# Issuing the dense products with the known block between the small scaling products, in the Schur and assembling stages

## The reference, cut to what matters

```python
def step(S, qkv):
    Qc, Kc, Vc = qkv
    G = Kc.T @ Kc + RIDGE_EPS * I
    W = jnp.linalg.solve(G, Kc.T @ Vc)
    U = U0
    for _ in range(POWER_K):
        U, _ = jnp.linalg.qr(W @ U)
    Wr = U @ (U.T @ W)
    S_new = DECAY_ALPHA * S + Wr
    out = SCALE * (Qc @ S_new)
    return (S_new, out)
```

## Time and profile before

| | before |
|---|---|
| device time, median of 3 runs | 1335.05 us (1333.93 to 1336.13) |
| device time of the profiled execution | 1337.31 us |
| its span in the trace | 1335.5 us |
| mean granted TensorE clock over the span | 0.866 of full |
| PE busy, share of the span | 74% |
| DVE busy | 84% |
| ACT busy | 50% |

### The profile page before, as it was taken

How to read it: one execution, slowest core, us unless ns; L and a number is a source line. 1 busy time by engine, 2 the same in 40 slices (tenths; PEclk the granted TensorE clock), 3 DMA queues, 4 the chain that set the end, 5 groups by cost and what they waited for, 6 DMA issues and landing times.

```text
span 1335.5 us, 41205 instructions
## 1 busy us (share of the span) xinstructions
PE 989.9 (74%) x17632; PEld 762.0 (57%) x17632; DVE 1118.0 (84%) x3452; ACT 661.8 (50%) x1392; POOL 174.6 (13%) x118
## 2 busy tenths in 40 slices
PE   1693017596687899897899897782499838998597
PEld 0463016555576667776767777672477625765254
DVE  6875996699999599999599999689889699764996
ACT  3683017555344567645467645352246515655254
POOL 2420123201011001011001111001200020001000
PEclk9897558798688899899799899796699958999799
DMA  4321003300000001110002110013112100111001
GB/s 149 104 99 38 0 0 129 127 25 17 3 4 3 3 18 33 35 51 3 4 10 73 34 36 3 4 31 129 33 36 71 51 30 18 48 48 32 8 17 32
DMA packets 42693, 53.04 MB, mean 40 GB/s; under 512 B 2992, under 2 KB 25600, under 8 KB 42512
## 3 DMA queue, kind: packets, MB, share of 16 engines
q1 hardware_dynamic: 42512, 50.42, 11.4%
HBM read 32.53 MB, written 17.87 MB: 38 GB/s over the span
## 4 chain that ended last, share of the span: by engine, by line
PE 54%; DVE 31%; ACT 9%; issue 4%; POOL 1%; DMA 0%; DVEq 0%; ACTq 0%; POOLq 0%
PE a_bank L547 7%; PE a_bank L618 6%; PE a_bank L707 5%; DVE a_outer L1564 4%; DVE a_total L1570 4%; DVE a_outer L1568 4%; DVE a_blocks L1573 4%; PE a_bank L713 3%; PE a_bank L697 3%; PE a_bank L561 3%; PE a_bank L832 3%; PE a_bank L817 3%; PE a_bank L799 3%; PE a_bank L643 2%; PE a_bank L769 2%
## 5 line engine op out<-in xcount | busy, mean ns | idle before, releaser
L987 ACT ACTIVATE a_work<-a_bank 128x512 f32<-128x512 f32 (+1 forms) x193 | 109.3, 606 | 180.9 <-PE a_bank L675 138.5
L1487 POOL TENSOR_TENSOR a_root<-a_recip,a_half 128x32 f32<-128x32 f32 (+2 forms) x24 | 89.8, 3742 | 592.7 <-DVEq L1559 575.2
L675 PE MATMUL a_bank<-a_ident,a_blocks 128*128 128x128 f32 x256 | 38.5, 318 | 134.6 <-DVE a_blocks L1584 134.6
L1564 DVE TENSOR_TENSOR a_outer<-a_blocks,a_weight 128x62 f32<-128x62 f32 (+15 forms) x248 | 129.6, 523 | 0.0
L1570 DVE TENSOR_REDUCE a_total<-a_outer 128x62 f32<-128x62 f32 (+30 forms) x248 | 127.2, 513 | 0.3
L987 ACT ACTIVATE a_solve<-a_bank 128x512 f32<-128x512 f32 (+2 forms) x184 | 88.0, 526 | 69.2 <-PE a_bank L713 52.9
L1568 DVE TENSOR_TENSOR a_outer<-a_blocks 128x60 f32<-128x60 f32 (+14 forms) x240 | 119.4, 497 | 0.0
L1573 DVE TENSOR_TENSOR a_blocks<-a_blocks,a_outer 128x60 f32<-128x60 f32 (+14 forms) x240 | 118.6, 494 | 0.0
L675 PEld LDWEIGHTS a_bank<-a_ident,a_blocks 128*128 128x128 f32 x256 | 37.1, 203 | 135.5 <-DVE a_blocks L1584 135.5
L618 PE MATMUL a_bank<-a_scaled,a_blocks 128*128 128x352 f32 x256 | 92.6, 505 | 13.1 <-ACT a_blocks L987 13.1
L987 ACT ACTIVATE a_scaled<-a_bank 128x512 f32<-128x512 f32 (+2 forms) x133 | 66.8, 528 | 57.9 <-PE a_bank L697 46.2
(11 more groups left out here) (198 smaller groups left out, 2232.0 us busy)
## 6 DMA issues: line engine op xcount, KB each, us to landing
a_pair<-in_L_attn_x SPq DMA_DIRECT2D x16, 256.0 KB, 3.0
s_base<-a_pair SPq DMA_DIRECT2D x16, 256.0 KB, 2.8
s_xnt<-a_xb SPq DMA_DIRECT2D x12, 256.0 KB, 2.0
s_c<-a_xc SPq DMA_DIRECT2D x12, 256.0 KB, 2.6
a_cg<-s_c SPq DMA_DIRECT2D x12, 256.0 KB, 2.8
a_cc<-s_c SPq DMA_DIRECT2D x12, 256.0 KB, 3.4
a_blocks<-s_base SPq DMA_DIRECT2D x12, 256.0 KB, 3.4
s_x<-a_xc SPq DMA_DIRECT2D x12, 256.0 KB, 2.0
```

The source lines that it names most:

```text
L987: nc.scalar.activation(out, view, ACT.Copy, scale=scale).then_inc(emptied, 1)
L1487: nc.gpsimd.tensor_tensor(root[:, :, a:b], recip[:, :, a:b], half[:, :, a:b], ALU.pow).then_inc(roots_ok, 1)
L1564: known = ch.inc(V.tensor_tensor(terms, m[:, :, i:HB, 0:i], bcast(weight[:, :, 0:i], 2, n_i), ALU.mult))
```

## The change

`scale_rows` and `squares` of the Tensor class become one generator, `solved`, that both stages use. For k = 0, 1, 2 the four dense products of part k (`known_into`) are no longer issued in one piece after the scaling of part k+1, but one at a time inside it: after its 16th, 32nd and 48th small product, and after its last. The dense products of the last part still come in one piece, since no scaling is left. Each dense product now takes its bank by itself, so it waits for that one bank instead of for four. The scaling of part k+1, the dense products and the squares of part k are now one step without a `yield` inside it (also on ACT, where one `yield` goes), so woven stages are cut in fewer, larger pieces. No product is added or removed.

```diff
@@ class Tensor
-            def scale_rows(self, k, stationary, moving):
...
-            def squares(self, k, half, mask, known):
-
-                four = self.u.fill(4, apart=True)
-                for c in range(4):
...
+            def solved(self, stationary, moving, half, mask, known):
...
+                def known_into(k, c):
+                    bank = self.u.fill(apart=True)
                     at = 32 * k + 8 * c
...
+                def scale(k, before):
+                    two, four = self.u.fill(2, apart=True), []
+                    for i in range(8):
+                        for c in range(4):
+                            for s in range(2):
+                                q = 32 * k + 8 * c + i
+                                last = nc.tensor.matmul(two[s][HB * c:HB * c + HB, i * DH:(i + 1) * DH], stationary(s, q), moving(s, q),
+                                                        start=True, stop=True)
+                        if before is not None and i % 2 == 1 and i < 7:
+                            four.append(known_into(before, i // 2))
+                    last.then_inc(filled, 2)
+                    if before is not None:
+                        four.append(known_into(before, 3))
+                    return four
+
+                mark = self.u.n + 2
+                scale(0, None)
+                yield
+                for k in range(parts):
+                    ready = mark
+                    if k + 1 < parts:
+                        mark = self.u.n + 2
+                        four = scale(k + 1, k)
+                    else:
+                        four = [known_into(k, c) for c in range(4)]
+                    self.u.need(ready, apart=True)
...
+                    last.then_inc(filled, 4)
+                    yield
                 return self.u.mark()
...
@@ class Scalar, solved
                 for k in range(NQ // 32):
                     if k + 1 < NQ // 32:
                         self.scale_rows(k + 1)
-                        yield
                     self.squares(k, dst, scale)
                     yield
```

More of the change, by code:

```diff
@@ L688, in lead_return @@
                 self.at["lead"] = self.u.mark()
-            def scale_rows(self, k, stationary, moving):
-                two = self.u.fill(2, apart=True)
-                for i in range(8):
-                    for c in range(4):
-                        for s in range(2):
-                            q = 32 * k + 8 * c + i
-                            last = nc.tensor.matmul(two[s][HB * c:HB * c + HB, i * DH:(i + 1) * DH], stationary(s, q), moving(s, q),
-                                                    start=True, stop=True)
-                last.then_inc(filled, 2)
-                return self.u.mark()
@@ L702, in squares @@
-            def squares(self, k, half, mask, known):
-                four = self.u.fill(4, apart=True)
-                for c in range(4):
+            def solved(self, stationary, moving, half, mask, known):
+                parts = NQ // 32
+                def known_into(k, c):
+                    bank = self.u.fill(apart=True)
                     at = 32 * k + 8 * c
-                    nc.tensor.matmul(four[c][:].rearrange("p (q z c) -> p q z c", z=2, c=HB)[:, :, half], mask[:], known[:, at:at + 8, :],
+                    nc.tensor.matmul(bank[:].rearrange("p (q z c) -> p q z c", z=2, c=HB)[:, :, half], mask[:], known[:, at:at + 8, :],
@@ L708, in squares @@
                                      start=True, stop=False, skip_group_check=True)
-                for i in range(8):
-                    for c in range(4):
-                        for s in range(2):
-                            both = scaled[HB * c:HB * c + HB, (2 * k + s) * 8 + i, :]
-                            last = nc.tensor.matmul(four[c][rows(s, None), i * DH:(i + 1) * DH], both, both, start=False, stop=True,
-                                                    skip_group_check=True)
@@ L715, in squares @@
-                last.then_inc(filled, 4)
+                    return bank
+                def scale(k, before):
[12 more added lines that the diff above has]
+                    return four
@@ new lines, in solved @@
+                mark = self.u.n + 2
[9 more added lines that the diff above has]
+                    self.u.need(ready, apart=True)
+                    for i in range(8):
+                        for c in range(4):
+                            for s in range(2):
+                                both = scaled[HB * c:HB * c + HB, (2 * k + s) * 8 + i, :]
+                                last = nc.tensor.matmul(four[c][rows(s, None), i * DH:(i + 1) * DH], both, both, start=False, stop=True,
+                                                        skip_group_check=True)
+                    last.then_inc(filled, 4)
+                    yield
@@ L745, in assemble @@
                 self.pe.sem_inc(schur_read, 1)
[L747 to L759 removed]
+                yield from self.solved(lambda s, q: work[rows(s, 1), q, :], lambda s, q: beside(kept[rows(s, 1), q, :], eyes[1][rows(s, 1)]),
+                                       0, minus[0], kept)
             def moments(self, src, mark):
```

25 lines of the change are left out of this document (2 added, 23 removed).

## The result

| | before | after |
|---|---|---|
| device time, median | 1335.59 us (1333.93 to 1339.07) | 1371.64 us (1364.94 to 1377.77) |
| device time of the profiled execution | 1337.31 us | 1374.81 us |
| mean granted clock over the span | 0.866 | 0.855 |

The ratio is 1.0265, with a 95% interval of 1.0208 to 1.0323: slower by 2.1 to 3.2%. The direction was forecast, the size was not: 1371.64 lies above the range of 1330 to 1366, and next to the time of the rival "Half clock holds", 1373.

A forecast was written before the change was run, and what follows sets the result against it. No engine bounds the whole; PE limits six stages, through code fetching (floor 7.2 us a part) and clock. 1337.31 + 0 + 14 (woven stages) = 1351.3, less 2.26 for the median: 1349 us, range 1330 to 1366.

The forecast's parts named there:

- Half clock holds: Rival: without long dense runs the clock stays down in straight and woven stages; +38 us, 1373 us; chance 0.13.
- the separate waits for each bank ... add no stop: At the dense products: the awaited banks were emptied by ACT during squares or first scaling products, so no cost.
- the sum of 14 us: Woven stages `assemble(1)` to `assemble(3)`: 3.15 + 2.2 + 0.8 - 1.5 = 4.65 us a stage, 14 us for three.
- the changes of shape: Entering, starting and leaving a dense run costs 0.35 us at full clock, 0.53 at half; three more a part.
- The wait for `xa`: Woven stages, first step c of `write`: a new wait of 2.2 us for ACT's copies.
- The 0.8 us: Woven stages, third step c of `write`: a new wait of 0.8 us behind ACT's copies of the second squares.
- The relief of 1.5 us: Woven stages: dense products ahead of the first stop and waits for ACT cover code fetching; -1.5 us a stage.
- I take the middle ... no change: Straight stages `schur(1)` to `schur(3)`: 30.6 us each, between full and half clock, beside 30.2 now.
- the bound of 4.5: Straight stages: upper end of the range, +4.5 us a stage. At half clock, last dense run and squares also 4.5.
- 9.4 was worked out: Straight stages: a part's work at half clock with the change takes 9.4 us, over the code floor of 7.2.
- `schur(0)` and `lead_return` took up what lay ahead of them: Gains or losses in `assemble(0)` and `schur(0)` go into PE's waits for DVE and count as nothing.
- The stops at the scaling line: Stops for "issue" should shrink in `assemble(1)` to `assemble(3)` and remain in the straight stages.

The follow-up runs named there:

- e11: Changed kernel with each part's four dense products in one run behind the scaling and one wait for all four banks; 12.4 us over the kernel before.
- e8: Changed kernel with dense products in one run and the `yield` back on both engines, so only the separate bank waits are left; 8.3 us over before.
- e12: Kernel before with three more copies of an already met wait, each with its semaphore increment, ahead of dense runs; 9.9 us over before.
- e1: Changed kernel with each part's four dense products in one run behind the scaling, separate bank waits and new `write` order kept; 20.0 us over before.
- e10: Changed kernel with `write` in one piece behind `assemble` in the last three assembling stages; 58.8 us over the kernel before.
- e9: Kernel before with `write` in one piece behind `assemble` in the last three assembling stages; 43.8 us over the kernel before.
- the halves: Two kernels, the change in the Schur stages alone and in the assembling stages alone; 12.2 and 18.9 us over the kernel before.
- e2: The change in the Schur stages alone, assembling stages as in the kernel before; 12.2 us over before.
- e4: Changed kernel with every dense product issued twice, the second overwriting the first; 44.5 us over the kernel before.
- e7: The change in the Schur stages alone, with the four dense products in one run after the scaling's 32nd small product; 8.9 us over before.

## Why the prediction was wrong, point by point

**What the loss is made of.** The order of `write` alone is 12.4 us (e11). The separate waits are 8.3 (e8) or 9.9 (e12) in kernels that spread nothing; the 7.6 between e1 and e11 agree, but the two intervals overlap. The spreading is 15.4 between the changed kernel and e1, 15.0 - 8 = 7 between e10 and e9, and some 10 from the halves (12.2 + 18.9 - 12.4 - 8.3). So 12 + 8 + 7 to 15 makes 27 to 35 of the 35.4. That the parts add up is assumed in this; the upper end comes out by itself, since 12.4 + 7.6 + 15.4 is the way from before over e11 and e1 to the changed kernel.

**A step that failed: "the separate waits for each bank ... add no stop".** I looked at whether the banks were free, and but for one wait of 1.3 us in `assemble(0)` they were. In kernels that spread nothing, the waits cost 8 to 10 us all the same. No rival had this.

**The woven stages: the sum of 14 us had no term for the clock.** It took the 0.92 of the earlier trace rows as given. The three stages lost 25.0 us by the profile. Of this the new waits for ACT are 6.7 us (2.11 + 1.24 + 1.24 at L897, 3 x 0.69 at L892; forecast 9.0), the changes of shape 27 x 0.22 = 5.9 at full clock (forecast 9.45), and the stops for "issue" gave back 9.8 - 6.6 = 3.2 (forecast 4.5). Each of these terms was forecast too high, and they leave some 16 us that the sum did not have. The clocks over the stages fell from 0.91, 0.88 and 0.92 to 0.80, 0.77 and 0.89; that this is where the 16 us went is shown in pieces for e11 only, in one stage.

**The order of `write`, priced without the clock.** The wait for `xa` was right: 2.2 us forecast for the first stage, 2.11 measured. In the trace after:

```profile
560.77 2.12 PE L732 MATMUL a_bank<-a_scaled 32*64 32x64 f32 x128
562.82 1.09 PE L883 MATMUL a_bank<-a_ident,a_xa 128*128 128x128 f32 x8
566.03 2.07 PE L897 MATMUL a_bank<-a_xa,a_xc 128*128 128x128 f32 x8 [2.11 <-ACT a_xa L983]
```

On ACT the copies that PE waited for:

```profile
562.93 2.06 ACT L983 ACTIVATE a_pair<-a_bank 128x512 f32<-128x512 f32 x4 [2.05 <-PE a_bank L732]
564.85 1.12 ACT L983 ACTIVATE a_xa<-a_bank 128x512 f32<-128x512 f32 x2
```

2.11 us at L897 in `assemble(1)` and 1.24 in the other two, and one more wait of 0.69 at L892. The 0.8 us that the prediction had for this one is 0.5 by its own rows (2.7 less two steps of about 1.1), and the copies of the squares, which were to hold it up, had ended before; PE waited for the copy of its own products, 0.60 us on ACT. What was missing is the clock: 4.15 us in e11's `assemble(1)`, in which PE fell to half clock once more behind the new wait. The relief of 1.5 us needs dense products ahead of the first stop, and e11 has none there (2.71 us). So its 12.4 us (7.7 to 17.1) stand against 3.0 a stage, 9.0 in all, which the interval includes.

**The straight stages: "I take the middle ... no change" failed.** They came out at +4.3 us each by the profile, beside the bound of 4.5; the two other profiles of the same Schur stages have +2.5 (e2) and +1.7 (e10), and the timed e2, with its waits, 12.2 in all. Where the mix of single dense and small products ran at half clock, its parts took 9.2 to 10.6 us (875.66 to 895.13 and 656.32 to 676.73 in the trace after), where 9.4 was worked out; what failed was the choice between the clocks. The bound itself was too low by its own rows: the last dense run and squares at half clock are 3.71 + 2.0 = 5.7 us, not 4.5. That the clock is a large part is shown by e4; e7 against e2 shows the clock, but no difference in time. How much spreading takes of the straight stages varies: 10.7 against e1, 6.0 between e10 and e9. In the changed kernel the last two straight stages have 2.4 and 1.2 us of stops for code left, where the kernel before had 4.2 and 5.0; my reading, not tried, is that work at half clock gives the code time.

**The shape changes** were priced too high (0.22 against 0.35 us, 0.38 against 0.53), which is 9 x 0.13 = 1.2 us a woven stage at full clock. The Trainium skill (TensorEngine Tiling (Array Packing), section Key Properties) says that a change of the tiling mode drains TensorE; the 0.22 us at full clock and 0.38 at half agree that such a change costs time.

**What held.** `schur(0)` and `lead_return` took up what lay ahead of them (L675 134.4 us, `schur(1)` 0.16 us later). ACT's waits at L897 and L892 appeared. The stops at the scaling line shrank in the woven stages, but against the forecast in the straight ones too.

**The rival that came true in number.** "Half clock holds" gave +13.5 straight and 24.8 woven; the profile has +12.8 and +25.0. Its mechanism is there in both, but the number is partly luck: it has nothing of the 8 to 10 us that the waits cost in the kernels without spreading, and other profiles of the same Schur stages lost 5.0 and 7.5 us where it has 13.5. Whether they still cost that in the changed kernel, where stops are fewer, was not tried.

## What to carry to other kernels

When small products share an engine with dense ones, read the granted clock of each stage before dissolving a dense run: a neighbour's work issued singly can leave PE at half clock, and here this weighed more than the changes of shape. When two steps are merged so that a `yield` goes, list what now stands next to what in the woven partner, and price the clock behind each new wait along with the wait. And where PE is short of code, a wait that was already met still had a price: ask once for several buffers.

## What the runs showed of the hardware that was not expected

96 waits that were already met, each with an increment, beside 41205 instructions, cost 9.9 us (6.1 to 13.5), 0.1 us each; in a row most start 0.15 us apart. All 22 long stops of PE for "issue" in the kernel before end 1.2 to 1.6 us after a code packet has landed. Twice the dense products, 22.8 us more work at full clock, took no more time in the three straight stages (106.3 us beside 104.2 to 112.0), where the clock was 1.00, 0.81 and 0.95 instead of 0.75, 0.58 and 0.57. PE busy 34.24 of 35.50 us was granted 0.57 of the clock: a busy PE did not by itself get 2.4 GHz.
